# First pass of a four-layer graph network: adjacency loaded in two halves, neighbour sum with the row sum outside, intermediates stored in another row order

## The reference

```python
h = jnp.maximum(_layernorm(x, axis=-1), 0.0)
A = adj + jnp.eye(N)
dis = A.sum(axis=-1) ** (-0.5)                  # 0 where the degree is 0
h_lin = jnp.einsum('bnd,hd->bnh', h, W) + b
out = jnp.einsum('bmn,bnh->bmh', dis[:, :, None] * A * dis[:, None, :], h_lin)
flat = out.reshape(B * N, H)                    # batch norm over all 32 graphs
flat = (flat - flat.mean(axis=0)) * rsqrt(flat.var(axis=0) + 1e-5) * bn_weight + bn_bias
x = x + relu(flat) + res_weight * h
```

## Time and profile before

| | |
|---|---|
| median of 3 runs (lowest to highest) | 4003.81 us (4001.38 to 4004.53) |
| the profiled execution, its own time | 4002.58 us |
| its span in the profile | 4000.6 us |
| instructions | 59388 |
| PE busy | 3707.4 us (93%) |
| DVE busy | 3095.1 us (77%) |
| ACT busy | 1996.0 us (50%) |
| POOL busy | 1565.6 us (39%) |
| DMA moved | 341.09 MB, mean 85 GB/s |
| granted TensorE clock, mean | 0.954 |

### The profile page before, as it was taken

How to read it: one execution, slowest core, us unless ns; L and a number is a source line. 1 busy time by engine, 2 the same in 40 slices (tenths; PEclk the granted TensorE clock), 3 DMA queues, 4 the chain that set the end, 5 groups by cost and what they waited for, 6 DMA issues and landing times.

```text
span 4000.6 us, 59388 instructions
## 1 busy us (share of the span) xinstructions
PE 3707.4 (93%) x19042; PEld 2704.5 (68%) x19042; DVE 3095.1 (77%) x5637; ACT 1996.0 (50%) x3047; POOL 1565.6 (39%) x980
## 2 busy tenths in 40 slices
PE   6899679999999999999999999999999999999986
PEld 6788445666777666667676667666677666666665
DVE  6777567888888888888888888888888888788752
ACT  4555245455555555545454545555555555555430
POOL 4565324343344444444333333343344444444310
PEclk9999779999999999999999999999999999999986
DMA  7888422222222222222222222222222222222200
GB/s 273 294 301 291 122 70 64 67 59 65 68 61 56 54 50 68 68 68 68 68 68 68 68 68 68 68 63 58 68 64 57 55 53 61 68 68 68 53 16 11
DMA packets 244574, 341.09 MB, mean 85 GB/s; under 512 B 28208, under 2 KB 129456, under 8 KB 244528
## 3 DMA queue, kind: packets, MB, share of 16 engines
q1 hardware_dynamic: 244528, 340.50, 30.8%
HBM read 188.89 MB, written 50.33 MB: 60 GB/s over the span
## 4 chain that ended last, share of the span: by engine, by line
PE 77%; DVE 10%; ACT 4%; issue 3%; DMA 2%; POOL 2%; SPq 1%; DVEq 0%; ACTq 0%; POOLq 0%
PE bank L1429 12%; PE bank L1480 12%; PE obank L1363 12%; PE bank L1220 9%; PE pair L1220 7%; PE pair L1347 7%; PE bank L1391 6%; PE bank L1448 3%; DVE minus_max L1020 3%; PE pair L1324 2%; DMA pT<-in_adjT 2%; PE obank L1252 2%; ACT hsq L619 1%; PE bank L1252 1%; DVE b_st L828 1%
## 5 line engine op out<-in xcount | busy, mean ns | idle before, releaser
L589 POOL TENSOR_TENSOR pT<-pT,node_edge 128x1024 f32<-128x1024 f32 x256 | 629.1, 2463 | 533.4 <-ACT pT L677 531.6
L677 ACT ACTIVATE pT<-pair 128x1024 f32<-128x1024 f32 x512 | 516.2, 1031 | 325.2 <-PE obank L1363 248.0
L1020 DVE TENSOR_REDUCE minus_max<-pair 128x2 f32<-128x1024 f32 x512 | 603.2, 1215 | 56.7 <-PE pair L1324 56.4
L1010 DVE TENSOR_TENSOR pT<-pT,node_edge 128x1024 f32<-128x1024 f32 x256 | 398.8, 1558 | 270.5 <-ACT pT L677 267.4
L1480 PEld LDWEIGHTS bank<-v,p3T 128*128 128x128 f32 x4096 | 502.6, 199 | 36.1 <-DVE p3T L1169 24.3
L1480 PE MATMUL bank<-v,p3T 128*128 128x65 f32 x4096 | 500.1, 280 | 19.9 <-DVE p3T L1169 19.9
L527 POOL TENSOR_TENSOR d_rs<-d_ve,minus_half 128x4 f32<-128x4 f32 x32 | 32.2, 1007 | 1208.1 <-DVE d_ve L840 1208.1
L1363 PE MATMUL obank<-pT,v 128*64 128x512 f32 x2048 | 490.1, 611 | 8.4 <-POOL pT L589 4.8
L1429 PE MATMUL bank<-w_s,hid 128*128 128x256 f32 x2048 | 479.5, 388 | 0.6 <-DVE hid L1099 0.6
L1429 PEld LDWEIGHTS bank<-w_s,hid 128*128 128x128 f32 x2048 | 382.6, 191 | 89.0 <-issue 40.2
L619 ACT ACTIVATE p3T<-x,d_sh,d_rs 128x256 f32<-128x256 f32 x128 | 66.4, 588 | 720.6 <-POOL d_sh L533 720.6
(11 more groups left out here) (189 smaller groups left out, 6430.9 us busy)
## 6 DMA issues: line engine op xcount, KB each, us to landing
pT<-in_adjT SPq DMA_DIRECT2D x32, 1024.0 KB, 5.5
a_at<-in_adjT SPq DMA_DIRECT2D x64, 512.0 KB, 3.7
q_parts<-high_parts SPq DMA_DIRECT2D x256, 128.0 KB, 4.8
k_parts<-high_parts SPq DMA_DIRECT2D x256, 128.0 KB, 4.1
b_at<-in_adjT SPq DMA_DIRECT2D x64, 512.0 KB, 3.9
hid<-in_x SPq DMA_DIRECT2D x32, 512.0 KB, 4.9
x_res<-hid SPq DMA_DIRECT2D x32, 512.0 KB, 5.7
pre_bn<-hsq SPq DMA_DIRECT2D x32, 512.0 KB, 4.9
```

The costliest lines, as they stand in the source:

```text
L589: nc.gpsimd.tensor_tensor(half, half, node_edge[:, 0:2, :], ALU.mult).then_inc(a_masked[0].sem, 1)
L677: nc.scalar.activation(dst, pair[p][:, :, :], func, **more).then_inc(a_copied[p].sem, 1)
L1010: nc.vector.tensor_tensor(half, half, node_edge[:, 2:4, :], ALU.mult).then_inc(a_masked[1].sem, 1)
L1020: nc.vector.tensor_reduce(minus_max[:, t, 2 * two_heads:2 * two_heads + 2], pair[p][:, :, :], AX.X, ALU.max, negate=True).then_inc(a_copie ...
```

## The change

`nodes` stays for the inputs and the output; the stores of `x_res` and `pre_bn` and the two loads that read them use `own`, in which partition p holds the four rows 4p to 4p + 3 of the DRAM tensor, one run of 4 KB. What each SBUF tile holds is as before; only the place in DRAM differs. `load_at` of the first pass becomes two loads of 512 KB: `load_at_low` (row blocks 0 and 1) waits for a new signal `c_agg_half` and stands last but one in SP's step with lead 2; `load_at_high` (row blocks 2 and 3) waits for `c_agg` and stands first with lead 1. `eye` waits for both. `aggregate` runs the row blocks k outside and the four outputs t inside, so all four are open at once, with one start and one stop for each bank; after k = 1 it raises `c_agg_half`.

```diff
+        def own(t, g):
+            return t[g.index()].rearrange("(p t) d -> p t d", t=T)
...
-        c_at_in = [signal(f"c_at_in{i}", 1, 16) for i in range(2)]
+        c_at_in = [signal(f"c_at_in{i}", 2, 16) for i in range(2)]
...
+        c_agg_half = signal("c_agg_half")
...
-            def load_at(g, par):
+            def load_at_low(g, par):
                 if not g.below(2):
+                    sp.wait_ge(*c_agg_half.upto(g.plus(-1), 0))
+                sp.dma_start(c_at[:, par, 0:K], nodes(adjT, g)[:, 0:K, :]).then_inc(c_at_in[par].sem, 16)
+            def load_at_high(g, par):
+                if not g.below(2):
                     sp.wait_ge(*c_agg.upto(g.plus(-1), 0))
-                sp.dma_start(c_at[:, par], nodes(adjT, g)).then_inc(c_at_in[par].sem, 16)
+                sp.dma_start(c_at[:, par, K:T], nodes(adjT, g)[:, K:T, :]).then_inc(c_at_in[par].sem, 16)
...
-                sp.dma_start(nodes(x_res, g), c_xres[:, par]).then_inc(c_xres_out[par].sem, 16)
+                sp.dma_start(own(x_res, g), c_xres[:, par]).then_inc(c_xres_out[par].sem, 16)
...
-                sp.dma_start(nodes(pre_bn, g), c_o[:, par]).then_inc(c_o_out[par].sem, 16)
+                sp.dma_start(own(pre_bn, g), c_o[:, par]).then_inc(c_o_out[par].sem, 16)
...
-            load_at(Graph(0), 0)
+            load_at_low(Graph(0), 0)
+            load_at_high(Graph(0), 0)
...
-            load_at(Graph(1), 1)
-            first_pass(sp, [(1, later(load_at)), (2, later(load_nat)), (-1, store_o), (4, later(load_x)), (2, store_res),
+            load_at_low(Graph(1), 1)
+            load_at_high(Graph(1), 1)
+            first_pass(sp, [(1, later(load_at_high)), (2, later(load_nat)), (-1, store_o), (4, later(load_x)), (2, store_res), (2, later(load_at_low)),
                             (0, load_rest)])
...
-                sp.dma_start(a_o[:, :, :], nodes(pre_bn, g)).then_inc(a_x_in.sem, 16)
+                sp.dma_start(a_o[:, :, :], own(pre_bn, g)).then_inc(a_x_in.sem, 16)
...
-                sp.dma_start(a_xr[:, :, :], nodes(x_res, g)).then_inc(a_x_in.sem, 16)
+                sp.dma_start(a_xr[:, :, :], own(x_res, g)).then_inc(a_x_in.sem, 16)
...
-                dve.wait_ge(*c_at_in[par].upto(g.half(), 1))
+                dve.wait_ge(*c_at_in[par].upto(g.half(), 2))
...
-                for t in range(T):
-                    dst = (obank if t < 2 else bank[2])[:, (t % 2) * D:(t % 2 + 1) * D]
-                    for k in range(T):
+                for k in range(T):
+                    for t in range(T):
+                        dst = (obank if t < 2 else bank[2])[:, (t % 2) * D:(t % 2 + 1) * D]
                         i = nc.tensor.matmul(dst, c_at[:, par, k, t * P:(t + 1) * P], c_hs[par][k // 2][:, k % 2, :],
-                                             start=k == 0, stop=k == T - 1)
+                                             start=k == 0 and t % 2 == 0, stop=k == T - 1 and t % 2 == 1)
+                    if k == K - 1:
+                        i.then_inc(c_agg_half.sem, 1)
                 i.then_inc(c_agg.sem, 1)
```

## The result

| | before | after |
|---|---|---|
| median | 4002.75 us (7 runs, 3996.86 to 4005.32) | 3987.68 us (7 runs, 3984.56 to 3993.89) |
| ratio, 95% interval | | 0.9965 (0.9955 to 0.9975) |
| profiled execution: span | 4000.6 us | 3982.8 us |
| start of the second pass (first step of `a_ln`) | 449.88 us | 432.58 us |
| from there to the end | 3550.7 us | 3550.2 us |

The change is worth 15.1 us by the medians, 0.35% by the ratio. All of it lies in the first pass: the span is 17.8 us shorter, the first pass 17.3 of them. (The profiled execution after was the quickest of its seven, 3984.56 us, 3.1 under their median; what follows on its trace is therefore a little on the good side.)

A forecast was written before the change was run, and what follows sets the result against it. It took the first pass's ring through the adjacency load to bound the kernel: -22.4 us for landings plus 1.0 for the start gives -21.4, 3981.2 on the profiled execution, 3982 as median; range 3966 to 3998.

The forecast's parts named there:

- What binds: First pass: the ring through the adjacency load is longest, 24.30 us for two graphs, falling to 22.7.
- 14 x 1.6 us for the landing: Adjacency landing falls from 5.4 to 3.8 us, 14 times in the chain: 22.4 us gained, 18 to 28 by the ends.
- the argument for 3.8: High half lands in 3.8 us, between 3.4 and 4.1, as the queue is nearly empty at issue (DMA share 0.10).
- rival 2: DMA queue 94% busy keeps most of the gain; high half lands in about 4.9 us; 3990 to 4002; chance 0.18.
- The other rings at 10.67 and 10.1 us: First pass: TensorE needs 10.67 us a graph, ScalarE, VectorE and GpSimd 10.1, both below the new 11.35.
- The start, 1 us: Two more loads on SP ahead of the loop cost 0 to 2 us, taken as 1.
- The low half on SP: nothing: One more SP issue of 0.37 us a step costs nothing, covered by SP's wait for the sum's end.
- rival 4: Low half held on SP behind load_x and store_res, so both halves go out together; 4003 us; chance 0.04.
- Rival 1: Ring falls to TensorE's floor, landing as in the quiet pass or better; to 3962, likely 3968; chance 0.12.
- The order of the sum: nothing: Row blocks outside, alternating open outputs on TensorE: zero cost, bounded at 1.3 us for 32 graphs.
- The layout: nothing on the path: Runs of 4 KB in place of 1 KB for stores and reads of 512 KB: 0 for the path.
- Rival 3: Slower: the split pays a DMA's fixed part twice, high half later than 5.4 us; about 4022 us; chance 0.05.

The follow-up runs named there:

- e9: Changed kernel with the store of x_res moved right behind the high half in SP's order; 3983.33 against 4007.44 us for the kernel before, ratio 0.9946.
- e5: Changed kernel with GpSimd's two batch-norm additions cut to four columns; 3984.90 us against 4004.03 us for the kernel before.
- e10: Changed kernel with the store of x_res and the load of x both moved behind the high half; 3982.76 against 4007.44 us for the kernel before, ratio 0.9942.
- e11: Changed kernel with store of x_res and load of x behind the high half, and VectorE's bias addition before its residual; 3980.48 against 4007.44 us (kernel before).
- e3: Kernel before with the sum's row blocks outside, four outputs open and one 1 MB load; 4004.01 against 4005.72 us for the kernel before, ratio 0.9999.
- e4: Changed kernel with both adjacency halves issued after the whole sum; 3998.78 against 4005.72 us for the kernel before, ratio 0.9985.

## Why the prediction was right, point by point

It gave 3982 us, 3966 to 3998, faster; 3987.68 was measured. Its gain of 21.4 us came out as 15.1.

*What binds.* Right: the ring through the adjacency load, seen 14 times before and 14 after, and nothing in the second pass. Of its signs, the turn shown above took 23.05 us (22.5 to 23 were forecast), but the mean over 100 to 390 us is two steps of 11.81, 23.6. VectorE's wait fell to 2.2 us a step, not to 1.4.

*14 x 1.6 us for the landing.* Close for the profiled execution: 82.8 - 61.7 = 21.1 us, 1.5 each. The level was off on both sides: it set 5.4 to 3.8, the chain had means of 5.9 and 4.4. That the difference came out is in part luck, for the argument for 3.8 does not hold. It was that the queue is nearly empty when the load is issued. But the load in that microsecond is the one issued at 276.19, which is not in the chain. The microsecond behind each of the three issues of the earlier trace rows's stretch, with the DMA share as the last but one number:

```profile
263.63:264.63 1.00, 1.00 (x11) 1.00 (x10) 0.73 (x4) 0.00 (x0) 0.60 (x1) 1.00 0.89 313
276.19:277.19 1.00, 1.00 (x10) 1.00 (x10) 1.00 (x2) 0.26 (x1) 0.92 (x3) 1.00 0.06 23
287.93:288.93 1.00, 1.00 (x11) 1.00 (x10) 0.76 (x3) 0.00 (x0) 0.77 (x1) 1.00 0.72 252
```

The two that the ring goes through (263.63, 287.93) had 0.89 and 0.72. Over all 14 of the chain the share is 0.49 in the mean before and 0.89 after, where the low half has gone out shortly before, as rival 2 had it. Whether that is what keeps the landing from 3.8 is open: `e9` has 0.42 and a mean of 4.4 all the same. The landings scatter from 3.49 to 5.56 in one execution, and the median run keeps 3 us less of the gain than the profiled one.

*The other rings at 10.67 and 10.1 us.* This is where the sum fell short: it put all else in the ring at nothing. In the profiled execution the first pass became 17.3 us shorter: 21.1 less for the landings, but some 5 us more for the residual and the bias addition in the chain (from 26 to 31), and 1.6 less for the rest. The 10.1 us were built without the residual and from durations of a kernel in which VectorE started it after GpSimd's additions. Once it starts earlier, the additions hold it up: 25 residuals of 1566 in place of 1280 ns are 7 us on VectorE in the stretch. The ring over GpSimd is thus 11.52, not 10.1, and the room that the prediction saw above 11.35 was not there. `e5` adds the caution: with the stall gone the time fell by no more than the final additions that went with it, as the landings grew. So the stall is shown, but not that it costs the missing microseconds by itself. SP's order alone (`e9`, `e10`) took some 9 us more off the medians, with intervals that still touch the change's, and the swap on top of it (`e11`) another 2.3.

*The start, 1 us.* The first landing in the chain begins at 52.48, at 51.22 before: 1.3 us.

*The low half on SP: nothing.* Right: it goes out 3.45 us ahead of the high one; rival 4 is out. Rival 1 is out too: the landing of the quiet pass (3.4) was not reached. *The order of the sum: nothing.* Right (`e3`). *The layout: nothing on the path.* Right alone (`e1`); with the split, not resolved. *Rival 3, the fixed part of a DMA, by the Trainium skill's rule to batch to 1 MiB ("DMA: Bandwidth & Descriptors", "Bandwidth").* Out: with both halves issued together (`e4`) the time is not above that of the whole. By that rule it should have been; for these overlapping transfers the measurement disagrees (3998.78 against 4005.72 us).

## What to carry to other kernels

Where a load waits for a buffer, cut it and start a part early. What that gives depends also on the order of the same queue, so put items that nobody waits for (a store, a far-ahead load) behind the urgent one, not ahead of it. A faster transfer starts its consumer earlier: look at what the other engines do at that new time, and rebuild the other rings from there. An edit that is right for one engine can lose because it shifts a DMA issue; test it with the queue's order changed too.

## What was not expected of the hardware

A VectorE instruction that reads two SBUF tensors (128 x 1024, float32, 1.28 us) all but stands still while GpSimd runs a two-input addition of the same size (2.36 us): 1.88 us with 0.80 us of overlap, 2.54 us with 1.46, the most in the changed kernel. VectorE's bias addition, which reads one input from PSUM, is not held up. In `e11` both parts of it run under the same GpSimd instruction, all but their last 0.20 us, and take 1.28 us for the two, as they do elsewhere:

```profile
238.56 2.37 POOL L559 TENSOR_TENSOR b_at<-b_at,p3T 128x1024 f32<-128x1024 f32 x1
...
239.85 1.28 DVE L910 TENSOR_TENSOR a_xbo<-pair,rden 128x512 f32<-128x512 f32 x2
```

A step with less data at its end is not quicker in proportion: of adjacency pieces of 1 MB, 512 KB and 256 KB after the sum, the chain's median landings were 5.6, 4.2 and 4.5 us, the means 5.9, 4.4 and 4.2. The pieces ahead of them differ too: 768 KB go out 1.9 us before the 256 KB, 512 KB go out 3.45 us before the 512 KB.
